# Attention steps whose weighted sums of V are given out in pairs, with a fourth buffer of probabilities

## The reference, cut to what matters

```python
scores = einsum('bhtd,bhsd->bhts', q, k) * scale      # then the causal mask
probs  = softmax(scores, axis=-1)
y      = einsum('bhts,bhsd->bhtd', probs, v)          # the weighted sums of V
x      = x + layernorm(y @ Wo + bo)                   # L0; L1 alike, with rotary q and k
```

## Time and profile before

| | us |
|---|---|
| median of three runs | 763.68 (763.57 to 765.76) |
| the profiled execution, its own time | 765.57 |
| span of its profile | 763.80 |
| mean granted TensorE clock over the span | 0.953 |

### The profile page before, as it was taken

How to read it: one execution, slowest core, us unless ns; L and a number is a source line. 1 busy time by engine, 2 the same in 40 slices (tenths; PEclk the granted TensorE clock), 3 DMA queues, 4 the chain that set the end, 5 groups by cost and what they waited for, 6 DMA issues and landing times.

```text
span 763.8 us, 13399 instructions
## 1 busy us (share of the span) xinstructions
PE 668.9 (88%) x4388; PEld 437.6 (57%) x4388; DVE 487.2 (64%) x1354; ACT 324.9 (43%) x684; POOL 249.0 (33%) x294
## 2 busy tenths in 40 slices
PE   3988999899568999999982978999998899999991
PEld 2633444344437899999962523444444456999870
DVE  4388788764683444444476789788866885344457
ACT  3654666465124333222241534666664231433322
POOL 3041112110137777444430084111101003677620
PEclk9999999899779999999995989999999999999995
DMA  3434210061008999999880245002000800499662
GB/s 100 138 118 137 74 36 1 1 197 53 27 1 263 342 311 323 301 312 315 260 267 0 75 146 159 24 18 101 2 1 1 268 32 23 149 291 308 214 213 84
DMA packets 60294, 108.60 MB, mean 142 GB/s; under 512 B 11194, under 2 KB 37131, under 8 KB 60100
## 3 DMA queue, kind: packets, MB, share of 16 engines
q1 hardware_dynamic: 52532, 93.86, 37.9%
q0 software_dynamic: 7632, 13.86, 5.6%
q10 hardware_dynamic: 64, 0.03, 0.0%
HBM read 79.98 MB, written 19.79 MB: 131 GB/s over the span
## 4 chain that ended last, share of the span: by engine, by line
PE 62%; DVE 23%; DMA 6%; issue 3%; ACT 3%; SPq 1%; POOL 1%; ACTq 0%; POOLq 0%; DVEq 0%
PE ps L1131 15%; PE ps L958 8%; DVE mx L1562 7%; PE ps L944 7%; PE ps L876 7%; PE ps L1144 5%; PE ps L1146 4%; PE ps L990 4%; DMA outs<-X,token 3%; DVE X L1959 2%; PE ps L1102 2%; PE ps L1070 1%; PE ps L831 1%; PE ps L909 1%; SPq L544 1%
## 5 line engine op out<-in xcount | busy, mean ns | idle before, releaser
L1562 DVE TENSOR_REDUCE mx<-ps 128x1 f32<-128x512 f32 (+3 forms) x304 | 184.3, 657 | 41.0 <-PE ps L879 22.5
L1300 ACT ACTIVATE X<-ps 128x1024 f32<-128x1024 f32 (+1 forms) x192 | 147.6, 809 | 86.8 <-PE ps L944 86.4
L876 PE MATMUL ps<-KA,QA 112*128 112x512 bf16 (+3 forms) x384 | 116.8, 339 | 10.6 <-DVE mx L1562 6.2
L762 POOL DMA_INDIRECT outs<-X,token x95 | 95.0, 1000 | 76.0 <-DVE X L1939 62.1
L734 POOL TENSOR_SCALAR_AFFINE_SELECT X<-X 128x512 f32<-128x512 f32 x64 | 40.7, 637 | 210.1 <-ACT X L1300 210.1
L944 PE MATMUL ps<-QA,KA 114*128 114x512 bf16 (+3 forms) x384 | 95.2, 331 | 2.4 <-ACT X L1300 1.2
L1131 PE MATMUL ps<-QA,KA 128*128 x756 | 95.0, 275 | 1.7 <-ACT QA L1406 1.7
L1131 PEld LDWEIGHTS ps<-QA,KA 128*128 128x128 f32 x756 | 92.0, 192 | 4.2 <-issue 2.4
L1926 DVE TENSOR_TENSOR X<-ps,X 128x128 f32<-128x128 f32 x95 | 27.7, 291 | 103.4 <-ACT X L1417 101.9
L754 POOL DMA_INDIRECT V<-token_rows,row_of_slot x64 | 65.7, 1026 | 70.4 <-DVE row_of_slot L1840 44.8
L876 PEld LDWEIGHTS ps<-KA,QA 112*128 112x128 bf16 x384 | 36.9, 98 | 89.4 <-DVE mx L1562 59.4
(11 more groups left out here) (298 smaller groups left out, 864.0 us busy)
## 6 DMA issues: line engine op xcount, KB each, us to landing
KA<-in_ex SPq DMA_DIRECT2D x95, 512.0 KB
X<-in_dn SPq DMA_DIRECT2D x95, 64.0 KB
outs<-empty SPq DMA_DIRECT2D x4, 1024.0 KB, 8.5
V<-outs SPq DMA_DIRECT2D x4, 1024.0 KB, 8.1
QA<-X SPq DMA_DIRECT2D x28, 128.0 KB, 2.5
KA<-X SPq DMA_DIRECT2D x28, 128.0 KB, 2.5
QA<-w_sdn SPq DMA_DIRECT2D x28, 128.0 KB, 2.5
KA<-parts_k SPq DMA_DIRECT2D x28, 128.0 KB, 2.5
```

Of the source, the lines that this page charges most:

```text
L762: pool.indirect_dma_start(out=outs[L], out_offset=bass.IndirectOffsetOnAxis(ap=token[L][:, i:i + 1], axis=0), in_=erows[:, g % OUT_RING, : ...
L876: mm = pe.matmul(ps[:, bank, j * w:(j + 1) * w], QA[0:KQ, h, i * P:(i + 1) * P], KA[0:KQ, h, s0:s0 + w], start=True, stop=not diag)
L1300: nc.scalar.activation(probs[:, st % PB, 2 * p:2 * p + 2, off:CH], ps[:, 4 + 2 * p:6 + 2 * p, off:CH], ACT.Exp, scale=SCALE).then_inc(S(f" ...
L1562: v.tensor_reduce(mx[:, part, i, h0:h0 + nh], ps[:, n % RB, 0:nh * w].rearrange("p (h w) -> p h w", h=nh), AX.X, ALU.max)\
```

## The change

`PB` becomes 4. In `schedule()` the even steps give out no `weigh` any more; each odd step `st` from 3 on gives out `weigh(st - 3)` and `weigh(st - 2)`, one behind the other, at the place where the one stood. The tile `X` is laid out anew for the fourth slot: it takes columns 6144 to 8191, where `pv_sb` and a part of the Q and K parts were, `pv_sb` moves to 8192, the bias parts to 9216, `cos_late` stays where it was. Since the fourth slot now covers Q and K parts of the first two groups, ACT waits before its first use (step 3) until the transfers that read them have landed.

```diff
-PB = 3
+PB = 4
...
-        if st >= HEAD_START:
-            out.append(("weigh", st - HEAD_START))
+        if st > HEAD_START and st % 2 == 1:
+            out += [("weigh", st - HEAD_START - 1), ("weigh", st - HEAD_START)]
         out += more
...
-        bias_parts = X[0:3 * 32, 7168:7168 + D].bitcast(BF16)
-        bias_left = X[0:1, 7424:7424 + 2 * D]
-        bias_mid = X[0:1, 7936:7936 + D].bitcast(BF16)
+        bias_parts = X[0:3 * 32, 9216:9216 + D].bitcast(BF16)
+        bias_left = X[0:1, 9472:9472 + 2 * D]
+        bias_mid = X[0:1, 9984:9984 + D].bitcast(BF16)
...
-        cos_late = X[:, PB * 2048:PB * 2048 + T]
+        cos_late = X[:, 6144:6144 + T]
...
                     act.wait_ge(S(f"sc{L}"), 2 * st + p + 1)
+                    if p == 0 and st == PB - 1:
+                        for x in range(2):
+                            act.wait_ge(S(f"qa_rows{L}_{x}"), 16 * 2 * NPROD)
                     if p == 0 and st >= PB:
                         act.wait_ge(S(f"pv{L}"), st - PB + 1)
```

## The result

The changed kernel takes 776.02 us (median of four runs, 773.55 to 777.35), the kernel before 764.72 beside it (763.57 to 767.29): 1.0126 times as long, 95% interval 1.0098 to 1.0154. That is 7.5 to 11.8 us, middle 9.6; forecast were +5.9 us and 769.6. It is slower, as forecast, and by more than forecast; the second rival's 762 to 766 us and the first's 755.5 are out. How far the reason is the one that the forecast gives is for the experiments to say.

A forecast was written before the change was run, and what follows sets the result against it. PE's own list was taken to bound the attention's middle; in the tails PE also waits for ACT. Middle +1.7 (L0), +1.5 (L1), tails +2.3 (L0), +0.4 (L1): +5.9 on 763.68, 769.6 us; 8 times in 10: 761.5 to 775.5.

The forecast's parts named there:

- second rival: Whole kernel: saving and new waits cancel, waits two thirds of those forecast or hidden by DVE's pace; 762 to 766 us, chance 0.12.
- first rival: Whole kernel: only the saved drains count, ACT answers in time; 46 x 0.22 less about 2, 755.5 us, chance 0.13.
- What a pair saves: PE, each paired `weigh`: one entry and exit fewer, 0.25 - 0.025 = 0.22 us; 46 groups fewer, 10.1 us.
- What the trip through ACT costs: Middle, behind wide even steps: next step's pair 1 can't start before 2.63 us; uncovered waits sum to 5.60 us a layer.
- the table's waits: Steps 6/7 to 34/35: PE's forecast waits for ACT by pair of steps, from 0 to 0.14 + 0.64 us.
- What costs nothing: Items put at no cost: ACT's step 3 wait, mask timing, queues, DVE's six 0.69 us maxima per two steps, three banked.
- DVE's maxima taking the place of the removed waits: Listed sign that the forecast is wrong: DVE's maxima become what PE waits for; no size given.
- waits for DVE taken as gone: Middle of a layer, last maximum before "rows" at steps 13 and 29: 0.9 of 1.0 us of waits vanish.
- pairs 3 and 5: Start of each layer's attention, two pairs each layer: DVE's maxima set the pace, so change taken as 0.
- The tails: Step 38 on: uncovered waits lengthen L0's tail by 2.3 us and L1's by 0.4 us.
- third rival: PE idles more, so its clock drops further, some 3.1 us each: one drop 772.7 us, two 775.8; chance 0.15.
- L0's bias stall: L0, DVE's bias work blocks PE until 142.84: step 30's `weigh` loses that cover, +0.2 us, making L0's middle +1.7.

## Why the prediction was right in its sign and short in its size

**What a pair saves: right.** 0.22 us forecast, 0.24 measured where nothing is in the way. The Trainium skill (TensorEngine Tiling (Array Packing), Key Properties) says that a change of tiling mode drains PE; the trace agrees, with the entry and exit that the forecast read from the earlier trace rows.

**What the trip through ACT costs: right.** In ten of the fifteen pairs 6/7 to 34/35 of L1 the net change is within 0.04 us of the table's waits less 0.22 (10/11: +0.53 against +0.56; 22/23: +0.42 against +0.45; 16/17: -0.24 against -0.22). With half the exponentials the first two become +0.05 and -0.07, so these waits are ACT's for the most part. Steps 6 to 36 came out at +1.94 us, forecast was +1.4 (the +1.5 for the middle without the 0.14 of 36/37). With the 3.58 us of saving, that is 5.5 us of new waits less those gone at DVE; forecast were 5.60 - 0.9 = 4.7.

**The step that failed: "What costs nothing", DVE's maxima.** "Three of them banked while the pair of sums runs" leaves out that the bank ring holds three units and no more: a DVE that empties it during the pair is behind for the rest of the two steps. "DVE's maxima taking the place of the removed waits", which the forecast lists as a sign of being wrong, came in part. The changed kernel's DVE in steps 30 and 31 of L1:

```profile
545.80 5.70 DVE L1565 TENSOR_REDUCE mx<-ps 128x1 f32<-128x512 f32 x9
552.27 1.29 DVE L1565 TENSOR_REDUCE mx<-ps 128x2 f32<-128x512 f32 x2 [0.78 <-PE ps L879]
```

Nine maxima without a pause, then 0.78 us of idling behind the pair that PE started at 550.08. These two steps cost +0.21 us, forecast was -0.22; they cost the same 0.21 with half the exponentials and save 0.21 with half the maxima too, so DVE is what holds them up. Of the 0.9 us of waits for DVE taken as gone, about 0.6 went (0.24 in steps 12 and 13, 0.34 in 28 and 29). Most of what was missed shows at the start, where pairs 3 and 5 were put at 0 because DVE sets the pace: steps 2 to 6 cost 0.69 us more in L0 and 0.65 in L1. In steps 4 and 5 a unit that the lone `weigh` gave DVE time for now finds no bank:

```profile
482.38 0.60 PE L944 MATMUL ps<-QA,KA 114*128 114x512 bf16 x2
483.17 0.39 PE L876 MATMUL ps<-KA,QA 112*128 112x512 bf16 x1 [0.20 <-DVE mx L1565]
```

In L1 those two steps cost 0.34 us with half the exponentials, still 0.21 with half the maxima and whole exponentials (with units moved from step 6 on), and save 0.25 only with both halved: here too either wait stands behind the other. The first rival's sentence from the same page of the Trainium skill (PSUM Bottleneck: once tiling has made TensorE four times as fast, copying out of PSUM may become the limit) fits, though no tiling was added here and the limit stands behind ACT rather than in its place: with the exponentials halved 2.2 of the 3.6 us are lost at DVE. The forecast put it in the tail and not in the middle of the trace before. But in the middle a unit waits 0.4 us for DVE's maxima, and the tail's 1.75 us are a wait for `xn`, which DVE computes from data in SBUF.

**The tails: right in both layers, 2.32 and 0.39 us with pairs there alone.** In the changed kernel L1's tail lost 2.0, and 1.6 of that is the fall of the clock, the third rival's mechanism: its price, put at 3.1 us a drop, is half that here. It came in both profiles of the changed kernel. It isn't a greater loss of clock overall: by the mean of 0.953 the clock costs at most (1 - 0.953) x 775.6 = 36.5 us over the span, and before (1 - 0.953) x 763.8 = 35.9.

**L0's bias stall: the clock, not the change.** Steps 32 to 36 became 1.0 us shorter, forecast was 0.6 longer. The windows over the stall's end, before and after:

```profile
142.00:150.00 8.00, 7.16 (x33) 2.35 (x34) 4.78 (x9) 3.67 (x4) 0.64 (x1) 0.57 0.00 0
```

```profile
142.00:150.00 8.00, 5.24 (x32) 2.13 (x32) 6.38 (x12) 4.25 (x5) 0.63 (x1) 0.79 0.00 0
```

By the granted clock (1 - 0.57) x 8.00 = 3.4 us went there before and (1 - 0.79) x 8.00 = 1.7 after. The version with single sums and the new layout also loses only 1.7 there and takes 13.95 us for steps 32 to 36 instead of 15.35; that with pairs in the tails alone, which has the same order up to step 37, has no fall there and takes 12.39. So the difference isn't the pairs' doing. Beside the 13.95 us, at the same loss of clock, the changed kernel's 14.32 are 0.4 more.

**Where 5.9 us became more.** The two profiled executions differ by 11.8 us. In the attention 8.4 stand against the forecast 5.9: 1.3 more at the start of the two layers, 0.5 in the middle of L1, 1.6 in L1's tail, and 1.0 less in the rest of L0 (1.6 less in the bias stall, 0.6 more in the other steps). The clock's 1.6 in L1's tail and 1.6 in the stall cancel by luck; what the sum was short by are the start and the middle, some 2.4 us, where DVE holds PE up, at the start beside ACT. The expert stage has the other 3.5, for which the forecast has no term; with the same pairs and moved units it had 0.7, so it doesn't come from the pairs alone. The timed ratio, 9.6 us, lies between the attention's part and the whole.

## What to carry to other kernels

Work that looks like a cost may be the cover of another engine's round trip: before grouping it, measure how long the trip is from issue to the next use (here 2.63 us) and whether what is left on the engine in between is longer. A gain of 0.24 us a group was hidden by two waits in line, ACT's and DVE's; removing one showed the other, so relieve both suspects together before a gain is called absent. Sort the groups by the trace, pair by pair, and keep those that gain: six pairs of 22 in a layer gave a version faster than both kernels, 2.6 us of it by the pairs themselves.

## What the runs showed that was not expected

Half of DVE's maxima left out, with the exponentials whole, makes even the changed kernel with moved units 1.4% faster than before, and steps 0 to 4 of L0 shrink by 4.2 us, of L1 by 1.4 with a fall of the clock in them: the start of each attention stage waits for DVE. A lone fall of the granted clock took 1.7 us by the clock, and what it cost depended on the place: 1.6 us in L1's tail, 0.64 in steps 2 to 4 of L1, where PE has idle time anyway (11.76 of 14.59 us busy with single sums and the new layout). It came at different places in different versions: in steps 2 to 4 of L1 in seven versions, but neither in the kernel before nor in the changed one. What brings it on there wasn't found.
